# A residual block on TensorE: x's column sum computed by VectorE, and part of the low parts formed by GpSimd

## The chip, the core and the metric

The kernel runs on one core of a Trainium2 chip. Times are microseconds (us) of that core; the time before is the median of three runs, 580.67 us (580.48 to 580.83). The change is judged against it.

## What is computed

For 32 images of 64 channels, 56 x 56 pixels, float32, two 3 x 3 convolutions with folded batch norm, the input added back, and a ReLU:

```
inv = gamma * rsqrt(var + EPS)          # per channel; bn(v) = v * inv + (beta - mean * inv)
out = relu(bn(conv3x3(x, w1), g1, b1, m1, v1))
out = bn(conv3x3(out, w2), g2, b2, m2, v2)
return relu(out + x)
```

## The kernel before, in words

Rows and columns are split into even and odd ones. Two row parities times 64 channels fill the 128 partitions; the two column parities are kept as two planes of 28 x 28 values in the free dimension. The three taps of a filter row are applied with the minimal filtering trick for two outputs at a time: of each input four derived tensors are formed, and each of these goes through its own matmul with a derived filter. Two of the four are called inner (t1, the sum of the odd and even plane, and t2, their difference), two are outer (differences of neighbours). For x they are `x_inner` and `x_outer`, for the hidden image `t_inner` and `t_outer`.

Precision is kept by splitting. ScalarE copies each derived tensor to a rounded high part (`x_hi`, `ti_hi`, `h_hi`, type fp32r), then a `tensor_tensor` subtracts it from the full one to give the low part (`x_lo`, `ti_lo`, `h_lo`). TensorE does three passes: high x high, high x low filters, low x high filters. The image is done in two halves of rows; PSUM holds for each half four banks: EVEN, ODD, SUM_T1 and SUM_T2. When the inner products of a half are there, ScalarE copies the t2 sum to `z` with both signs (`copy_sum`), and VectorE's `join` writes T1 + z into EVEN and ODD at once. Then TensorE adds the outer products onto these banks, and ScalarE's ReLU reads them (`relu_hidden`, L555, for the first convolution, `relu_out`, L587, for the second). ScalarE's `residual` (L525) puts x's inner tensors into the second convolution's sum banks before the products.

The loop has one step per image. Step s does, on each engine and in a fixed order written out by hand, parts of the first convolution of image s and of the second of images s-1 and s-2. The order on TensorE in a step: for each half the inner products of conv 1 (image s) and the outer products of conv 2 (image s-2); then for each half the inner products of conv 2 (image s-1) and the outer of conv 1 (image s). The first of these, half 0 of conv 1's inner products, writes the sum bank that the join of conv 2, image s-2, half 0 reads, and waits for it (`joined[2]`). Engines talk through counting semaphores; some waits are written as `wait_ge` ahead of an instruction, and in the printed orders a row `ISA` or `REGISTER_ALU` carries such a wait or computes the count that it waits for.

VectorE in a step (lines of the kernel before): `sum_hidden` L407, join L398 (conv 2, s-2, half 1), `difference_hidden` L414, low part of t1 L430, join (conv 1, s, half 0), low part of t2, `outer_hidden` L422, `difference_x` L369 (image s+1), join (conv 1, s, half 1), `outer_x` L376, low part of h L430, inner low part of x L384, join (conv 2, s-1, half 0), outer low part of x L384.

x comes in by two ways. SyncE loads the whole image, both planes, to `x_sb`. The sum of the planes isn't computed by an engine: SyncE loads the even plane once more, to `x_inner[:, k, 0]` (`load_even`, L263), and GpSimd issues a second transfer of the odd plane which adds to it on the way (`add_odd`, L300, `accum_op=ALU.add`). There are four buffers of it (TBUFS). Only image 0's sum is made by VectorE (L354). GpSimd's computing is otherwise the prologue: scaling and summing the second layer's filters (L317, L179 to L181).

## Time and profile before

| | |
|---|---|
| median of 3 runs | 580.67 us |
| the profiled execution | 580.64 us, its span 579.0 us |
| TensorE busy | 567.1 us, 98% of the span |
| VectorE busy | 546.2 us, 94% |
| ScalarE busy | 493.1 us, 85% |
| GpSimd busy | 37.2 us, 6% |
| granted TensorE clock, mean | 0.997 |
| DMA | 79.20 MB, mean 137 GB/s |

The profile is that of one execution. Its page gives busy times, the chain of work that ended last, and groups of instructions; the trace behind it also answers for single instructions with start and duration. Consecutive instructions of an engine can overlap by up to a tenth of a microsecond, so a busy share near 100% doesn't say by itself that an engine sets the pace.

### The profile page before, as it was taken

To read this page: it belongs to the slowest core of one execution; us is meant where nothing else is said; L and a number is where in the kernel's file an instruction comes from. 1 tells how busy PE (TensorE), PEld (TensorE's weight loads), DVE (VectorE), ACT (ScalarE), POOL (GpSimd) and SP (SyncE) were. 2 spreads that over 40 slices of the span, in tenths; PEclk is the share of its full clock that TensorE was granted. 3 is DMA by queue.
4 is the path that set the end of the run, shared out by engine and by line. 5 is a ranking of instruction groups with operands and counts; after the bars stand their busy time and mean duration, and the time that the engine had idled before them with its cause. 6 is when DMAs were issued, how large, how long until landed. Compare 5 with 4: busy or idle time off the path is not lost.

```text
span 579.0 us, 9009 instructions
## 1 busy us (share of the span) xinstructions
PE 567.1 (98%) x3058; PEld 543.4 (94%) x3058; DVE 546.2 (94%) x462; ACT 493.1 (85%) x744; POOL 37.2 (6%) x44
## 2 busy tenths in 40 slices
PE   7889999999999999999999999999999999999997
PEld 4569999999999999999999999999999999999997
DVE  6799999999999999999999999999999999999985
ACT  3488888998888998888998888998888998888985
POOL 6200000000000000000000000000000000000000
PEclk9899999999999999999999999999999999999999
DMA  8733455544445544455544455544455544451112
GB/s 263 199 103 110 132 144 149 165 146 121 130 143 150 163 145 120 131 143 150 163 145 115 137 143 152 162 140 129 127 143 150 163 150 122 128 144 46 39 57 111
DMA packets 31407, 79.20 MB, mean 137 GB/s; under 512 B 2592, under 2 KB 19104, under 8 KB 31392
## 3 DMA queue, kind: packets, MB, share of 16 engines
q1 hardware_dynamic: 26784, 66.05, 31.5%
q0 software_dynamic: 4464, 12.89, 14.5%
q8 instruction: 9, 0.15, 0.1%
q10 hardware_dynamic: 144, 0.07, 0.1%
q14 instruction: 6, 0.05, 0.0%
HBM read 53.31 MB, written 25.69 MB: 136 GB/s over the span
## 4 chain that ended last, share of the span: by engine, by line
PE 93%; DVE 3%; ACT 2%; issue 1%; DMA 1%; ACTq 0%
PE psum L664 93%; DMA bn<-params_dram 1%; DVE x_lo L384 1%; ACT x_hi L515 1%; DVE psum L398 1%; DVE w_lo L198 0%; DVE t_outer L358 0%; DVE x_inner L369 0%; ACT hidden L555 0%; ACT psum L525 0%; ACT w_hi L193 0%; DVE t_inner L414 0%; DVE x_inner L354 0%; DVE x_inner L352 0%; DVE inv L337 0%
## 5 line engine op out<-in xcount | busy, mean ns | idle before, releaser
L664 PE MATMUL psum<-x_hi,w_hi 128*128 128x420 f32 x496 | 172.3, 347 | 0.5 <-DVE w_lo L198 0.5
L664 PE MATMUL psum<-x_hi,w_lo 128*128 128x420 f32 x496 | 168.8, 340 | 0.0
L664 PE MATMUL psum<-x_lo,w_hi 128*128 128x420 f32 x496 | 168.5, 340 | 0.0
L398 DVE TENSOR_TENSOR psum<-psum,z 128x784 f32<-128x784 f32 (+1 forms) x128 | 127.1, 993 | 3.6 <-ACT hidden L555 1.6
L664 PEld LDWEIGHTS psum<-x_hi,w_hi 128*128 128x128 f32 x496 | 93.1, 188 | 6.4 <-issue 4.0
L664 PEld LDWEIGHTS psum<-x_hi,w_lo 128*128 128x128 f32 x496 | 93.2, 188 | 0.8
L664 PEld LDWEIGHTS psum<-x_lo,w_hi 128*128 128x128 f32 x496 | 93.2, 188 | 0.5
L555 ACT ACTIVATE hidden<-psum,bias,half_inv 64x56 f32<-64x56 f32 (+2 forms) x128 | 84.5, 687 | 5.9 <-PE psum L664 4.7
L664 PE MATMUL psum<-h_hi,w_hi 128*128 128x392 f32 x256 | 87.3, 341 | 0.0
L664 PE MATMUL psum<-h_hi,w_lo 128*128 128x392 f32 x256 | 87.2, 341 | 0.0
L664 PE MATMUL psum<-h_lo,w_hi 128*128 128x392 f32 x256 | 87.1, 340 | 0.0
L664 PE MATMUL psum<-ti_hi,w_hi 128*128 128x392 f32 x248 | 86.7, 350 | 0.0
L664 PE MATMUL psum<-ti_lo,w_hi 128*128 128x392 f32 x248 | 84.5, 341 | 0.0
L587 ACT ACTIVATE out_sb<-psum 128x784 f32<-128x784 f32 x63 | 52.1, 827 | 38.0 <-PE psum L664 38.0
L664 PE MATMUL psum<-ti_hi,w_lo 128*128 128x392 f32 x248 | 84.1, 339 | 0.0
L525 ACT ACTIVATE psum<-x_inner 128x392 f32<-128x392 f32 x128 | 59.2, 501 | 15.1 <-DVE psum L398 15.1
L535 ACT ACTIVATE ti_hi<-t_inner 128x812 fp32r<-128x812 f32 (+2 forms) x64 | 54.6, 857 | 11.0 <-DVE t_inner L407 10.9
L430 DVE TENSOR_TENSOR ti_lo<-t_inner,ti_hi 128x812 fp32r<-128x812 f32 (+2 forms) x64 | 61.9, 970 | 0.0
L430 DVE TENSOR_TENSOR h_lo<-t_outer,h_hi 128x1624 fp32r<-128x1624 f32 (+2 forms) x33 | 59.2, 1795 | 0.4 <-ACT h_hi L535 0.4
L422 DVE TENSOR_TENSOR t_outer<-hidden 128x1624 f32<-128x1624 f32 (+2 forms) x33 | 59.2, 1793 | 0.0
L384 DVE TENSOR_TENSOR x_lo<-x_outer,x_hi 128x1568 fp32r<-128x1568 f32 x31 | 55.3, 1785 | 3.3 <-ACT x_hi L515 3.3
L376 DVE TENSOR_TENSOR x_outer<-x_sb 128x1624 f32<-128x1624 f32 x31 | 57.1, 1843 | 0.0
(62 smaller groups left out, 809.6 us busy)
## 6 DMA issues: line engine op xcount, KB each, us to landing
x_sb<-x_dram SPq DMA_DIRECT2D x32, 814.0 KB, 4.8
out_dram<-out_sb SPq DMA_DIRECT2D x63, 392.0 KB, 2.8
x_inner<-x_dram SPq DMA_DIRECT2D x31, 406.0 KB, 3.2
x_inner<-x_dram POOLq DMA_DIRECT2D x31, 406.0 KB, 5.0
out_dram<-out_sb SPq DMA_DIRECT2D x2, 196.0 KB, 2.3
z<-w_dram SPq DMA_DIRECT2D x1, 384.0 KB, 3.7
out_sb<-w_dram SPq DMA_DIRECT2D x1, 384.0 KB, 6.3
bn<-params_dram ACTq DMA_DIRECT2D x1, 68.0 KB, 3.9
```

What stands on the lines that cost most here:

```text
L376: nc.vector.tensor_tensor(x_outer[:], runs(cells, 0, XPLANE), runs(cells, 1, XPLANE), ALU.subtract).then_inc(tx_ready["outer"], 1)
L384: nc.vector.tensor_tensor(x_part(x_lo, k, places), full, x_part(x_hi, k, places).bitcast(F32), ALU.subtract).then_inc(xlo_ready[which], 1)
L398: nc.vector.tensor_tensor(psum[:, half, EVEN:ODD + 1, 0:width], t1, z[:, half, :, 0:width], ALU.add).then_inc(joined[conv], 1)
L422: nc.vector.tensor_tensor(t_outer[:, :, rows], hid_cols[:, :, rows, 0:WQ], hid_cols[:, :, rows, 1:WQ + 1], ALU.subtract).then_inc(th_ready ...
L430: nc.vector.tensor_tensor(lo, full, hi.bitcast(F32), ALU.subtract).then_inc(hlo_ready[which], 1)
L515: nc.scalar.activation(x_part(x_hi, k, places), full, ACT.Copy).then_inc(xhi_ready[which], 1)
L525: ins = nc.scalar.activation(psum[:, half, bank, 0:width].rearrange("p (j q) -> p j q", q=WQ), x_full("inner", k)[0][:, i, j0:j1], ACT.Cop ...
L535: nc.scalar.activation(hi, full, ACT.Copy).then_inc(hhi_ready[which], 1)
L555: return nc.scalar.activation(hid_data[rows, :, pairs, 0:WQ], sums[rows], ACT.Relu, bias=bias[rows, 0:1], scale=half_inv[rows, 0:1])
L587: nc.scalar.activation(out_sb[:, half], psum[:, half, EVEN:ODD + 1, 0:(j1 - j0) * WQ], ACT.Relu).then_inc(out_ready, 1)
L664: ins = nc.tensor.matmul(sums, w[:, i, far, :], t[:, j0:j1, 0:WQ], start=not onto and at == 0, stop=at == len(todo) - 1, skip_group_check= ...
```

## The change

x's sum for each image is computed by VectorE (`sum_x`, 784 elements per partition), behind the join of conv 1, half 1, and ahead of `outer_x`. Both transfers that made it are gone. In exchange VectorE forms only rows 0 to 14 of the outer low parts of x and of h (for h, but for the last two images). The rest, 13 rows of x (364 elements) and 14 rows of h (392), is done by GpSimd in four instructions per image, one for each of the two outer tensors ("place") of x and of h. Before each, GpSimd waits for the semaphores that one of VectorE's joins waits for and for the VectorE instruction ahead of that join (`beside_join`). TensorE, and VectorE where it overwrites the full tensor, wait for the pieces (`x_piece`, `h_piece`).

```diff
-            def load_even(n, k):
-                sp.dma_start(x_inner[:, k, 0], x_rows[n][:, 0:RUN]).then_inc(even_in[k], 16)
...
-                if not isinstance(s, int) or 0 <= s < N - 3:
-                    wait(sp, res_ready, 2 * s)
-                    load_even(s + 3, (k + 3) % 4)
...
-            def add_odd(n, k):
-                pool.wait_ge(even_in[k], landed(n, k))
-                odd = x_rows[n][:, XPLANE + 1:XPLANE + 1 + RUN]
-                pool.dma_start(x_inner[:, k, 0], odd, accum_op=ALU.add).then_inc(summed[k], 16)
...
+            def x_part_low(n, k, place):
+                rows = slice(HALF1[1][0], NQ)
+                pool.wait_ge(xhi_ready["outer"], n)
+                pool.tensor_tensor(x_lo[:, k % 2, place, rows], x_full("outer", k)[0][:, place, rows],
+                                   x_hi[:, k % 2, place, rows].bitcast(F32), ALU.subtract).then_inc(x_piece, 1)
+            def hidden_part_low(n, b, place):
+                rows = slice(HALF1[1][0], NP)
+                pool.wait_ge(hhi_ready["outer"], n + 1)
+                pool.tensor_tensor(h_lo[:, b, place, rows], t_outer[:, place, rows],
+                                   h_hi[:, b, place, rows].bitcast(F32), ALU.subtract).then_inc(h_piece, 1)
+            def beside_join(conv, n, half, earlier, count):
+                pool.wait_ge(earlier, count)
+                pool.wait_ge(z_ready[conv], 2 * n + half + 1)
+                pool.wait_ge(inner[conv], 2 * (2 * n + half) + 2)
...
             def step(s, k):
-                if there_is(s, s + 2):
-                    add_odd(s + 2, (k + 2) % 4)
+                now, last, store = there_is(s, s), there_is(s, s - 1), there_is(s, s - 2)
+                if is_step(s, N) or is_step(s, N + 1):
+                    return
+                if store:
+                    beside_join(2, s - 2, 1, th_ready["t1"], s)
+                    pool.wait_ge(hidden_ready, 2 * (s - 1) + 2)
+                    hidden_part_low(s - 2, k % 2, 1)
+                if now and not is_step(s, 0):
+                    if not is_step(s, 1):
+                        beside_join(1, s, 0, hlo_ready["t1"], s - 1)
+                        pool.wait_ge(out_ready, 2 * (s - 2) + 1)
+                    x_part_low(s, k, 0)
+                    if not is_step(s, 1):
+                        beside_join(1, s, 1, th_ready["outer"], s)
+                        pool.wait_ge(out_ready, 2 * (s - 2) + 2)
+                    x_part_low(s, k, 1)
+                if last and not is_step(s, N - 1):
+                    beside_join(2, s - 1, 0, xlo_ready["inner"], s + 1)
+                    pool.wait_ge(hidden_ready, 2 * s + 1)
+                    hidden_part_low(s - 1, (k + 1) % 2, 0)
...
+            def sum_x(n, k):
+                cells = runs(x_sb[:, k % XBUFS], 0, XPLANE + 1).rearrange("p s (j c) -> p s j c", c=WQ + 1)
+                nc.vector.tensor_tensor(x_full("inner", k)[0][:, 0], cells[:, 0, :, 0:WQ], cells[:, 1, :, 0:WQ],
+                                        ALU.add).then_inc(sum_ready, 1)
...
                 wait(dve, xlo_ready["outer"], n - 1)
+                wait(dve, x_piece, 2 * (n - 1))
...
+                rows = slice(0, NQ if which == "inner" else HALF1[1][0])
                 dve.wait_ge(xhi_ready[which], n)
-                nc.vector.tensor_tensor(x_part(x_lo, k, places), full,
-                                        x_part(x_hi, k, places).bitcast(F32),
+                nc.vector.tensor_tensor(x_part(x_lo, k, places)[:, :, rows], full[:, :, rows],
+                                        x_part(x_hi, k, places)[:, :, rows].bitcast(F32),
...
                 wait(dve, hlo_ready["outer"], n)
+                wait(dve, h_piece, 2 * (N - 2) if is_step(n, N - 1) else 2 * n)
...
+                if which == "outer" and half is None and not is_step(n, N - 2):
+                    rows = slice(0, HALF1[1][0])
+                    full, hi, lo = full[:, :, rows], hi[:, :, rows], lo[:, :, rows]
...
                     difference_x(1, 1)
+                    sum_x(1, 1)
                     join(1, 0, 0, (2, -2))
                     outer_x(1, 1)
...
                 if ahead:
+                    sum_x(s + 1, ka)
                     outer_x(s + 1, ka)
                 if last:
...
                 if which == "inner":
-                    act.wait_ge(summed[k], landed(n, k))
+                    act.wait_ge(sum_ready, n + 1)
...
                 pe.wait_ge(joined[conv], 2 * n + half + 1)
+                if half == 1 and conv == 1 and not is_step(n, 0):
+                    pe.wait_ge(x_piece, 2 * n)
+                if half == 1 and conv == 2 and not is_step(n, N - 2) and not is_step(n, N - 1):
+                    pe.wait_ge(h_piece, 2 * n + 2)
```

Line numbers shift: the join is L421 after the change, the sum of the hidden planes L430, its difference L437, t_outer L446, the low parts L457 (hidden) and L407 (x), x's difference L384, x_outer L398. The first place to see is VectorE in a step of the loop, from the outer hidden tensor to the outer low part of x. Before:

```order
L422 TENSOR_TENSOR t_outer<-hidden 128x1624 [waits hlo_outer]
L366 ISA
L369 TENSOR_TENSOR x_inner<-x_sb 128x28x28 [waits res_ready,x_in0]
L393 REGISTER_ALU
L394 ISA [waits z1_ready]
L398 TENSOR_TENSOR psum<-psum,z 128x2x392 [waits out_ready,inner1]
L376 TENSOR_TENSOR x_outer<-x_sb 128x1624 [waits xlo_outer]
L430 TENSOR_TENSOR h_lo<-t_outer,h_hi 128x1624 [waits hhi_outer]
L384 TENSOR_TENSOR x_lo<-x_inner,x_hi 128x1568 [waits xhi_inner]
L398 TENSOR_TENSOR psum<-psum,z 128x2x392 [waits hidden_ready,inner2,z2_ready]
L384 TENSOR_TENSOR x_lo<-x_outer,x_hi 128x1568 [waits xhi_outer]
```

After:

```order
L446 TENSOR_TENSOR t_outer<-hidden 128x1624 [waits h_piece,hlo_outer]
L381 ISA
L384 TENSOR_TENSOR x_inner<-x_sb 128x28x28 [waits res_ready,x_in0]
L416 REGISTER_ALU
L417 ISA [waits z1_ready]
L421 TENSOR_TENSOR psum<-psum,z 128x2x392 [waits out_ready,inner1]
L390 TENSOR_TENSOR x_inner<-x_sb 128x28x28
L398 TENSOR_TENSOR x_outer<-x_sb 128x1624 [waits x_piece,xlo_outer]
L457 TENSOR_TENSOR h_lo<-t_outer,h_hi 128x2x420 [waits hhi_outer]
L407 TENSOR_TENSOR x_lo<-x_inner,x_hi 128x1568 [waits xhi_inner]
L421 TENSOR_TENSOR psum<-psum,z 128x2x392 [waits hidden_ready,inner2,z2_ready]
L407 TENSOR_TENSOR x_lo<-x_outer,x_hi 128x2x420 [waits xhi_outer]
```

One instruction is new, the sum (L390), between the join of half 1 and x_outer. The two outer low parts are 2 x 420 elements long in place of 1624 and 1568, and t_outer and x_outer wait for pieces too. No instruction changed its place among the others.

The second place is GpSimd's queue in the loop. Before, two steps:

```order
L300 ISA [waits even_in0]
L300 DMA x_inner<-x_dram 128x812
L298 REGISTER_ALU
L300 ISA [waits even_in1]
L300 DMA x_inner<-x_dram 128x812
```

After, one step and the beginning of the next (z1, z2: `z_ready`; hlo_t1, th_outer, xlo_inner, th_t1: the VectorE instruction ahead of the join):

```order
L315 ISA [waits z2_ready,th_t1]
L308 TENSOR_TENSOR h_lo<-t_outer,h_hi 128x392 [waits hhi_outer,hidden_ready,inner2]
L314 ISA [waits hlo_t1]
L315 ISA [waits z1_ready]
L301 TENSOR_TENSOR x_lo<-x_outer,x_hi 128x364 [waits xhi_outer,out_ready,inner1]
L314 REGISTER_ALU [waits th_outer]
L315 ISA [waits z1_ready]
L301 TENSOR_TENSOR x_lo<-x_outer,x_hi 128x364 [waits xhi_outer,out_ready,inner1]
L313 REGISTER_ALU
L308 TENSOR_TENSOR h_lo<-t_outer,h_hi 128x392 [waits hidden_ready,inner2,hhi_outer,z2_ready,xlo_inner]
```

Where a step had one transfer, it has four tensor_tensor instructions, with rows that wait or compute counts between them.

## Rows read from the trace of the kernel before

**Rows 1.** The page, busy time of the engines.
```profile
PE 567.1 (98%) x3058; PEld 543.4 (94%) x3058; DVE 546.2 (94%) x462; ACT 493.1 (85%) x744; POOL 37.2 (6%) x44
```

**Rows 2.** Windows table, one step: us, then each engine's busy time.
```profile
core 0: us, PE busy (x) PEld busy (x) DVE busy (x) ACT busy (x) POOL busy (x), PEclk, DMA share, GB/s
302.50:319.83 17.33, 17.33 (x97) 16.99 (x97) 16.87 (x15) 15.32 (x25) 0.82 (x2) 1.00 0.47 127
```

**Rows 3.** Timeline, TensorE: first matmuls of steps (start us, us).
```profile
41.91 0.46 PE L664 MATMUL psum<-x_hi,w_hi 128*128 128x420 f32 x1 [0.53 <-DVE w_lo L198]
...
302.50 0.43 PE L664 MATMUL psum<-x_hi,w_hi 128*128 128x420 f32 x1
...
337.22 0.43 PE L664 MATMUL psum<-x_hi,w_hi 128*128 128x420 f32 x1
...
545.50 0.42 PE L664 MATMUL psum<-x_hi,w_hi 128*128 128x420 f32 x1
```

**Rows 4.** Timeline, VectorE, one step and the next one's join.
```profile
305.42 0.98 DVE L398 TENSOR_TENSOR psum<-psum,z 128x784 f32<-128x784 f32 x1
...
306.31 1.00 DVE L414 TENSOR_TENSOR t_inner<-hidden 128x812 f32<-128x812 f32 x1
...
308.16 1.04 DVE L398 TENSOR_TENSOR psum<-psum,z 128x840 f32<-128x840 f32 x1
...
310.02 1.85 DVE L422 TENSOR_TENSOR t_outer<-hidden 128x1624 f32<-128x1624 f32 x1
...
312.66 0.98 DVE L398 TENSOR_TENSOR psum<-psum,z 128x784 f32<-128x784 f32 x1
...
321.87 1.00 DVE L407 TENSOR_TENSOR t_inner<-hidden 128x812 f32<-128x812 f32 x1 [0.43 <-ACT hidden L555]
...
336.10 0.98 DVE L398 TENSOR_TENSOR psum<-psum,z 128x784 f32<-128x784 f32 x1
```

**Rows 5.** Timeline, ScalarE, the same step.
```profile
311.36 0.83 ACT L587 ACTIVATE out_sb<-psum 128x784 f32<-128x784 f32 x1 [0.41 <-PE psum L664]
...
312.08 1.56 ACT L535 ACTIVATE h_hi<-t_outer 128x1624 fp32r<-128x1624 f32 x1
...
315.31 1.52 ACT L515 ACTIVATE x_hi<-x_inner 128x1568 fp32r<-128x1568 f32 x1
...
320.37 1.37 ACT L555 ACTIVATE hidden<-psum,bias,half_inv 64x56 f32<-64x56 f32 x2
```

**Rows 6.** VectorE's groups by form: count | busy us, mean ns | idle before.
```profile
L430 DVE TENSOR_TENSOR h_lo<-t_outer,h_hi 128x1624 fp32r<-128x1624 f32 x31 | 57.2, 1846 | 0.4 <-ACT h_hi L535 0.4
...
L384 DVE TENSOR_TENSOR x_lo<-x_outer,x_hi 128x1568 fp32r<-128x1568 f32 x31 | 55.3, 1785 | 3.3 <-ACT x_hi L515 3.3
...
L369 DVE TENSOR_TENSOR x_inner<-x_sb 128x784 f32<-128x784 f32 x31 | 30.6, 987 | 0.0
...
L430 DVE TENSOR_TENSOR h_lo<-t_outer,h_hi 128x840 fp32r<-128x840 f32 x1 | 1.0, 1027 | 0.0
```

**Rows 7.** Timeline, GpSimd, prologue.
```profile
6.97 0.53 POOL L306 TENSOR_TENSOR inv<-inv,bn 128x66 f32<-128x66 f32 x1 [4.61 <-DVE inv L342]
...
8.04 0.20 POOL L308 TENSOR_TENSOR bias<-bn,inv 128x2 f32<-128x2 f32 x1
...
9.85 1.84 POOL L317 TENSOR_TENSOR out_sb<-out_sb,half_inv 128x768 f32<-128x768 f32 x1
...
14.01 1.58 POOL L180 TENSOR_TENSOR w_mat<-out_sb 128x256 f32<-128x256 f32 x1
...
15.56 1.45 POOL L181 TENSOR_TENSOR w_mat<-out_sb 128x256 f32<-128x256 f32 x1
```

**Rows 8.** Timeline, VectorE, prologue.
```profile
6.66 0.23 DVE L342 TENSOR_TENSOR inv<-inv,tmp 128x66 f32<-128x66 f32 x1
...
9.87 3.47 DVE L358 TENSOR_TENSOR t_outer<-x_sb 128x1568 f32<-128x1568 f32 x1
...
14.94 1.49 DVE L369 TENSOR_TENSOR x_inner<-x_sb 128x784 f32<-128x784 f32 x1
...
16.35 1.03 DVE L398 TENSOR_TENSOR psum<-psum,z 128x840 f32<-128x840 f32 x1
```

More of the change, by code:

```diff
@@ L110, in residual_block @@
         wlo_ready = {1: sem("wlo1"), 2: sem("wlo2")}
-        first_sum = sem("first_sum")
-        even_in = [sem(f"even_in{i}") for i in range(TBUFS)]
-        summed = [sem(f"summed{i}") for i in range(TBUFS)]
+        sum_ready = sem("sum_ready")
+        x_piece, h_piece = sem("x_piece"), sem("h_piece")
         tx_ready = {"inner": sem("tx_inner"), "outer": sem("tx_outer")}
@@ L199, in low_weights @@
                               ALU.subtract).then_inc(wlo_ready[conv], 1)
-        def landed(n, k):
-            return (n - k) * (16 // TBUFS) + (16 if k else 0)
         def runs(cells, first, step):
@@ L259, in store @@
                 sp.dma_start(out_rows[n][:, half], out_sb[:, half]).then_inc(stored[half], 16)
-            def load_even(n, k):
-                sp.dma_start(x_inner[:, k, 0], x_rows[n][:, 0:RUN]).then_inc(even_in[k], 16)
             sp.dma_start(w_raw[1], w1).then_inc(w_in[1], 16)
             load(sp, 0, 0)
-            load_even(1, 1)
             sp.dma_start(w_raw[2], w2).then_inc(w_in[2], 16)
             load(sp, 1, 1)
-            load_even(2, 2)
             def step(s, k):
@@ L309, in _ @@
             pool.tensor_tensor(bias[:], bn[:, 2 * COLS:2 * COLS + 2], bias[:], ALU.subtract).then_inc(bias_ready, 1)
-            add_odd(1, 1)
             pool.wait_ge(w_in[2], 16)
@@ L354, in first_x @@
                 nc.vector.tensor_tensor(planes[:, 0], cells[:, 0, :, 0:WQ], cells[:, 1, :, 0:WQ],
-                                        ALU.add).then_inc(first_sum, 1)
+                                        ALU.add).then_inc(sum_ready, 1)
                 cells = x_sb[:, 0, 0:2 * XPLANE].rearrange("p (s r) -> p s r", s=2)[:, :, 0:RUN] \
@@ L370, in difference_x @@
                                         ALU.subtract).then_inc(tx_ready["inner"], 1)
+            def sum_x(n, k):
+                cells = runs(x_sb[:, k % XBUFS], 0, XPLANE + 1).rearrange("p s (j c) -> p s j c", c=WQ + 1)
+                nc.vector.tensor_tensor(x_full("inner", k)[0][:, 0], cells[:, 0, :, 0:WQ], cells[:, 1, :, 0:WQ],
+                                        ALU.add).then_inc(sum_ready, 1)
             def outer_x(n, k):
                 wait(dve, xlo_ready["outer"], n - 1)
+                wait(dve, x_piece, 2 * (n - 1))
                 cells = x_sb[:, k % XBUFS]
@@ L743, in step @@
                             pe.wait_ge(prep[1], 3)
-                            pe.wait_ge(first_sum, 1)
+                            pe.wait_ge(sum_ready, 1)
                         sum_products(1, half, 1, SUM_T1, whole_passes(1, 1), False).then_inc(inner[1], 1)
```

## The prediction

> **What bounds the kernel now.** The first view is the page's list of busy times: TensorE is busy for 98% of the span [rows 1]. A change that touches no matmul then looks as if it could do nothing. The windows table of one step of the loop in the middle says more: TensorE is busy all the time and VectorE for 16.87 of 17.33 us [rows 2]. Two engines are full, so the question is which one waits, and TensorE's waits are too short to show as idle time. They are found in the starts of the matmuls. The first matmul of a step starts at 41.91 in step 2 and at 545.50 in step 31 [rows 3]: 29 steps, 503.59 us, 17.365 us a step.
>
> Then I read VectorE, ScalarE and TensorE side by side and look for the chain that closes on itself. It spans two steps:
> - step start 302.50 [rows 3]; TensorE reaches the end of the half that ScalarE's output ReLU waits for, and that ReLU starts at 311.36;
> - ScalarE then has no idle time until its ReLU of 320.37 ends at 321.74 [rows 5];
> - VectorE starts on the hidden image at 321.87 and works without idle time up to the join that starts at 336.10 and ends at 337.08 [rows 4];
> - the step after next starts at 337.22 [rows 3], 0.14 later. That matmul overwrites the bank that the join read.
>
> 337.22 - 302.50 = 34.72 = 2 x 17.36. So the loop runs at the length of this chain, not at TensorE's rate. What lengthens VectorE's part of it by D adds D/2 to each step. What shortens VectorE's work outside it adds and saves nothing.
>
> A second, shorter loop lies next to it: VectorE's t_outer (310.02 + 1.85 = 311.87) releases ScalarE's h_hi, which starts at 312.08 because the output ReLU before it is in the way [rows 4, 5]. About 0.2 us of delay is free there.
>
> **The change part by part.** *VectorE's own work.* One more sum of 784 elements: 987 ns like its twin, of which 0.09 overlaps a neighbour (a join of 0.98 is followed after 306.31 - 305.42 = 0.89) [rows 4, 6]: +0.90. h_lo falls from 1624 to 840 elements: 1846 to 1027 ns, -0.82. The outer x_lo falls from 1568 to 840: 1785 to about 1030 ns, -0.76 [rows 6]. In sum -0.68 us of load per step. But the sum and h_lo lie ahead of the join that closes the chain, and the outer x_lo behind it, where VectorE waits for the hidden ReLU anyway. On the chain it is +0.90 - 0.82 = +0.08.
>
> *The four pieces on GpSimd* (392, 364, 364, 392 elements). GpSimd does hardly anything in the loop, so its own time is free. What it does to VectorE isn't. In the prologue both work at once. GpSimd's scaling starts at 9.85 and ends at 11.69; VectorE's t_outer, started at 9.87, took 3.47 us, where 1568 elements take 1.785 [rows 6 to 8]: 1.69 longer, that is the overlap of 1.82 less 0.13. VectorE's x_inner at 14.94 took 1.49 instead of 0.97 (the mean of the other 30, from [rows 6]) and GpSimd's sum before it ended at 15.59: 0.65 of overlap, 0.52 longer, again 0.13 less. But the join at 16.35 took 1.03, its usual length (1.04 at 308.16), while GpSimd worked from 16.43 to 17.01 [rows 4, 7, 8]. So a VectorE operation on two SBUF tensors waits for GpSimd, and a join, which reads PSUM and z, doesn't. A piece is free as long as it ends within its join, plus 0.13.
>
> Does it? GpSimd's speed: after VectorE let it go at 14.94 + 1.49 = 16.43, 256 elements were done at 17.01, 2.27 ns each [rows 7, 8]. 364 elements are 0.83 us, 392 are 0.89. An operation of two elements took 0.20 [rows 7], so a fixed 0.10 to 0.20 comes on top; I take 0.15. When does it start? Its first wait is for the VectorE operation ahead of the join, which ends 0.08 after the join starts (16.43 and 16.35). From VectorE's end to GpSimd's start it took 6.97 - 6.89 = 0.08 [rows 7, 8]; VectorE itself took 0.13 behind ScalarE (321.87 after 321.74) [rows 4, 5]. The piece has three to four further waits queued behind the first, already met; I take 0.12, between 0.08 and 0.30. A piece of h then ends 0.08 + 0.12 + 0.15 + 0.89 = 1.24 after the join's start. The next VectorE operation, a difference or low part of two SBUF tensors each time, starts at 0.89 and bears 0.13: 0.22 to 0.24 late. A piece of x at the 784-element join: 1.18 - 1.02 = 0.17. At the longer join (1.04): 0.10. From both sides: 0.16, 0.09 and 0 with the small values, 0.46, 0.40 and 0.29 with the large.
>
> Three of the four lie on the chain (h beside 305.42, x beside 308.16, x beside 312.66): 0.24 + 0.10 + 0.17 = 0.51. The fourth, beside the join of 336.10, lies behind the chain and is hidden in VectorE's wait. Before t_outer there are 0.34, of which some 0.2 are free; that loop, 17.16 + 0.34 = 17.50, stays below the other.
>
> The chain grows by 0.08 + 0.51 = 0.59, the step by 0.295, to 17.66; over 29 steps 8.6 us. With the small values: 0.33, 4.8 us. With the large: 1.23, 17.8 us.
>
> The Trainium skill (SBUF — State Buffer, Who interferes with whom) says the same of who waits, but that the second one to issue "fully blocks until the first finishes". By that rule the 0.13 are not borne and each of the three blocks is 0.13 longer: 29 x 0.39 / 2 = 5.7 us more, about 597. The trace disagrees by those 0.13, twice, so the sum above stands without it.
>
> *The transfers.* The loads of the even half and GpSimd's accumulating loads go. TensorE waits for none of them in the loop, and VectorE's operations are no shorter when they don't run; nothing. ScalarE's inner x_hi now waits for VectorE's sum, which ends 0.34 + 0.17 + 0.88 after 313.64, at 315.0; ScalarE comes to that x_hi at 315.31 [rows 5]. Hidden by 0.3. New waits: TensorE needs a piece at the second half of the outer products, some 5 us after the x piece and 2 to 3 after the h piece; outer_x on VectorE stands a sum behind its piece. Nobody waits there. SP's queue loses waits and gets none.
>
> *The start.* Image 1's sum comes directly behind x_inner (14.94). GpSimd's last filter sum, which until now ran beside the join of 16.35, now blocks that sum by 0.52: 0.88 + 0.52 = 1.4, all on the way to TensorE's outer products. In step 1 the two x pieces have no join beside them, come together with VectorE's outer x_lo and hold VectorE up by about 0.75 each, less the 0.76 saved: +0.7. A last 0.3 beside the filters' low part. Sum 2.4; from both sides 0.9 (only the sum) to 3.5. Nothing at the end, where pieces and sums have stopped.
>
> Sum: 580.64 (span 579.0 and 1.64 around it; the median of the runs shown is 580.67) + 8.6 + 2.4 = 591.6.
>
> **The rivals.**
> 1. *The join covers the pieces.* GpSimd is quick to start and has no fixed cost (2.27 ns x 364 is well under a join). Then the chain grows by 0.08 only: 29 x 0.04 = 1.2, with a start of 0.9 to 2.4: 583. For it speaks that 0.22 us per piece rests on two numbers of 0.1 each; against it, that the small measured values already give 0.33.
> 2. *GpSimd is late.* Its queue walks through register arithmetic and waits before each piece; if that takes 0.35 and more, blocks are 0.35 to 0.45 each: 29 x (0.08 + 1.05) / 2 = 16.4, with 3 at the start 600. Were the pieces not beside the joins at all, that is if the change doesn't do what it says, VectorE's load would be 16.87 - 0.68 + 3.44 = 19.63 a step, 2.27 more: about 648.
> 3. *Faster: VectorE's load decides.* If VectorE's total and not the two-step chain sets the step, 0.68 saved is worth something, as soon as blocks stay under 0.17 a piece. TensorE's own floor is near: its first matmul starts 0.07 to 0.14 behind the join, and it can gain at most some 0.11 a step, 29 x 0.11 = 3.2; with 0.9 at the start 578.4. For it: VectorE is 97% busy [rows 2]. Against it: it is idle 0.43 before 321.87, each step, waiting for ScalarE [rows 4].
>
> **How the numbers follow.** Forecast 0.62, rival 1 0.15, rival 2 0.13 (0.03 of it far out), rival 3 0.10. The likeliest case alone is 585 to 598: from 4.8 with 0.9 to 14 with 3. The range takes in rival 1 and the near part of rival 2: 582.5 to 601. A measurement of this kernel tells about 0.2% (1.2 us) from no change: slower 0.85 (forecast, rivals 1 and 2 but for some 0.05), same 0.07, faster 0.08.
>
> **What would show it.** In the profile after: steps of 17.66 between first matmuls; joins of unchanged length; the operation behind each of the four joins 0.1 to 0.25 longer than its form (the differences of x and h, the low part of t2 above 1.00, the outer x_lo above 1.03); VectorE's idle time ahead of the hidden sum at about 0.7 us instead of 0.43 (17.66, less 16.92 - 0.68 + 0.74); pieces of about 1.0 us starting 0.2 behind a join. Wrong if those operations keep their lengths (rival 1), or if the idle time before the hidden sum doesn't grow while the step shrinks (rival 3). The time would also be wrong if the chain had a partner that I take for free, h_hi above all.

## The result, and the profile after

The changed kernel takes 592.35 us (592.04 to 592.53, 4 runs) against 580.61 (580.48 to 580.83, 4 runs): 1.0206 times as long, 95% interval 1.0192 to 1.022. Forecast were 591.6, range 582.5 to 601.

The page of the changed kernel, busy times, against [rows 1]:

```profile
PE 571.4 (97%) x3058; PEld 543.2 (92%) x3058; DVE 547.2 (93%) x493; ACT 494.7 (84%) x744; POOL 141.3 (24%) x135
```

As many matmuls as before, almost the same VectorE time (547.2 against 546.2), and 11.1 us more span. The busy times don't tell where it went. TensorE's first matmuls of step 2, 3, 26 and 31 do (timeline, start and duration; against [rows 3]):

```profile
43.28 0.46 PE L693 MATMUL psum<-x_hi,w_hi 128*128 128x420 f32 x1 [0.71 <-DVE w_lo L197]
...
60.76 0.43 PE L693 MATMUL psum<-x_hi,w_hi 128*128 128x420 f32 x1
...
468.73 0.43 PE L693 MATMUL psum<-x_hi,w_hi 128*128 128x420 f32 x1 [0.15 <-DVE psum L421]
...
555.92 0.43 PE L693 MATMUL psum<-x_hi,w_hi 128*128 128x420 f32 x1
```

The span of 590.1 against 579.0 falls in three parts. Up to step 2: 43.28 against 41.91, +1.37. The 29 steps to step 31: 512.64 us, 17.677 each against 17.365, +9.05. After it: 34.18 against 33.50, +0.68. And the 29 are of two kinds. Of the 24 in the loop, the first (step 2) took 17.48 and the other 23 average 17.738 ((468.73 - 60.76) / 23); the five behind the loop, whose instructions are written out, average only 17.438.

VectorE's groups by form in the changed kernel (count | busy us, mean ns | idle before), against [rows 6]:

```profile
L457 DVE TENSOR_TENSOR ti_lo<-t_inner,ti_hi 128x812 fp32r<-128x812 f32 x60 | 64.2, 1070 | 0.0
...
L437 DVE TENSOR_TENSOR t_inner<-hidden 128x812 f32<-128x812 f32 x31 | 40.2, 1298 | 0.0
L407 DVE TENSOR_TENSOR x_lo<-x_outer,x_hi 128x840 fp32r<-128x840 f32 x31 | 38.2, 1232 | 3.1 <-ACT x_hi L544 3.1
L421 DVE TENSOR_TENSOR psum<-psum,z 128x840 f32<-128x840 f32 x32 | 33.1, 1034 | 0.7 <-PE psum L693 0.6
L457 DVE TENSOR_TENSOR h_lo<-t_outer,h_hi 128x840 fp32r<-128x840 f32 x31 | 31.6, 1021 | 0.0
L430 DVE TENSOR_TENSOR t_inner<-hidden 128x812 f32<-128x812 f32 x31 | 31.4, 1014 | 22.5 <-ACT hidden L584 22.5
...
L390 DVE TENSOR_TENSOR x_inner<-x_sb 128x784 f32<-128x784 f32 x31 | 30.3, 976 | 0.0
```

The hidden difference (L437) takes 1298 ns where it took 995 (it was 1.00 in [rows 4]). The outer x_lo takes 1232 where the h_lo of the same 840 elements takes 1021. The low parts of t1 and t2 (L457) average 1070 against 997, and single rows show that those of t1 are all 0.99, so t2's are longer by twice the difference. The joins kept their length. The new sum (L390) is not longer than its twin. Behind three of four joins something blocks VectorE, behind one nothing. VectorE's idle time before the hidden sum rose to 22.5 us in all, where it was 12.4; that is 0.73 a step in the loop against 0.44.

The pieces on GpSimd, one step of the changed kernel, and VectorE's rows around them:

```profile
325.86 1.03 POOL L308 TENSOR_TENSOR h_lo<-t_outer,h_hi 128x392 fp32r<-128x392 f32 x1 [5.49 <-DVE x_lo L407]
329.99 1.04 POOL L308 TENSOR_TENSOR h_lo<-t_outer,h_hi 128x392 fp32r<-128x392 f32 x1 [3.10 <-DVE t_inner L430]
333.15 0.90 POOL L301 TENSOR_TENSOR x_lo<-x_outer,x_hi 128x364 fp32r<-128x364 f32 x1 [2.12 <-DVE ti_lo L457]
337.00 1.32 POOL L301 TENSOR_TENSOR x_lo<-x_outer,x_hi 128x364 fp32r<-128x364 f32 x1 [2.95 <-DVE t_outer L446]
```

```profile
328.56 1.01 DVE L430 TENSOR_TENSOR t_inner<-hidden 128x812 f32<-128x812 f32 x1 [0.77 <-ACT hidden L584]
329.49 0.97 DVE L421 TENSOR_TENSOR psum<-psum,z 128x784 f32<-128x784 f32 x1
330.37 1.53 DVE L437 TENSOR_TENSOR t_inner<-hidden 128x812 f32<-128x812 f32 x1
...
336.59 0.96 DVE L384 TENSOR_TENSOR x_inner<-x_sb 128x784 f32<-128x784 f32 x1
337.48 0.97 DVE L421 TENSOR_TENSOR psum<-psum,z 128x784 f32<-128x784 f32 x1
338.36 0.96 DVE L390 TENSOR_TENSOR x_inner<-x_sb 128x784 f32<-128x784 f32 x1
```

The piece at 329.99 starts 0.42 after VectorE's hidden sum ended (329.57). It ends at 331.03, which is 0.66 after the hidden difference began; that one is longer by 0.53, again 0.13 less. The last piece is the exception: it has 1.32 us on record, more than any other, and blocks nobody. It started at 337.00, before its join, found the port (so the shared access to SBUF is called here, for which the two engines wait for each other) taken by x's difference (336.59 to 337.55) and was through 0.77 us after that. A piece that stands ready doesn't pay the time from VectorE's signal, and it is through 0.13 sooner than one of the same size that starts on a free port (0.90). It comes in so early because it waits for t_outer, not for the instruction directly ahead of its join (the diff shows `th_outer`; the order has the x difference between them), which the forecast missed.

### The profile page after: what moved, and what is told of

Its sections match the earlier page's. It is cut to its first block, busy times and chain, and to the rows that moved or that the text cites. A ratio compares the mean times of both kernels' runs of the same rounds, so it can differ in the third digit from the quotient of the medians.

```text
span 590.1 us, 9394 instructions
## 1 busy us (share of the span) xinstructions
PE 571.4 (97%) x3058; PEld 543.2 (92%) x3058; DVE 547.2 (93%) x493; ACT 494.7 (84%) x744; POOL 141.3 (24%) x135
## 4 chain that ended last, share of the span: by engine, by line
PE 49%; DVE 22%; issue 15%; ACT 13%; DMA 1%; DVEq 1%; ACTq 0%
PE psum L693 49%; DVE psum L421 6%; ACT hidden L584 4%; DVE t_outer L446 4%; ACT x_hi L544 3%; DVE ti_lo L457 3%; DVE x_outer L398 2%; ACT z L577 1%; DVE x_inner L390 1%; ACT z L578 1%; ACT psum L554 1%; DVE h_lo L457 1%; DVE x_lo L407 1%; DVE t_inner L437 1%; DMA bn<-params_dram 1%
## 5 line engine op out<-in xcount | busy, mean ns | idle before, releaser
L421 DVE TENSOR_TENSOR psum<-psum,z 128x784 f32<-128x784 f32 (+1 forms) x128 | 126.4, 987 | 3.5 <-ACT hidden L584 1.6
L308 POOL TENSOR_TENSOR h_lo<-t_outer,h_hi 128x392 fp32r<-128x392 f32 x60 | 62.3, 1038 | 258.1 <-DVE x_lo L407 172.5
L301 POOL TENSOR_TENSOR x_lo<-x_outer,x_hi 128x364 fp32r<-128x364 f32 x62 | 68.0, 1097 | 162.0 <-ACT out_sb L616 72.9
L457 DVE TENSOR_TENSOR ti_lo<-t_inner,ti_hi 128x812 fp32r<-128x812 f32 (+2 forms) x64 | 66.3, 1039 | 0.0
L446 DVE TENSOR_TENSOR t_outer<-hidden 128x1624 f32<-128x1624 f32 (+2 forms) x33 | 59.0, 1787 | 0.0
L398 DVE TENSOR_TENSOR x_outer<-x_sb 128x1624 f32<-128x1624 f32 x31 | 56.9, 1837 | 0.0
```

The costliest lines, as they stand in the source:

```text
L301: pool.tensor_tensor(x_lo[:, k % 2, place, rows], x_full("outer", k)[0][:, place, rows], x_hi[:, k % 2, place, rows].bitcast(F32), ALU.sub ...
L308: pool.tensor_tensor(h_lo[:, b, place, rows], t_outer[:, place, rows], h_hi[:, b, place, rows].bitcast(F32), ALU.subtract).then_inc(h_piec ...
L398: nc.vector.tensor_tensor(x_outer[:], runs(cells, 0, XPLANE), runs(cells, 1, XPLANE), ALU.subtract).then_inc(tx_ready["outer"], 1)
L421: nc.vector.tensor_tensor(psum[:, half, EVEN:ODD + 1, 0:width], t1, z[:, half, :, 0:width], ALU.add).then_inc(joined[conv], 1)
L446: nc.vector.tensor_tensor(t_outer[:, :, rows], hid_cols[:, :, rows, 0:WQ], hid_cols[:, :, rows, 1:WQ + 1], ALU.subtract).then_inc(th_ready ...
L457: nc.vector.tensor_tensor(lo, full, hi.bitcast(F32), ALU.subtract).then_inc(hlo_ready[which], 1)
```

## The experiments

The two theories: **A**, the step is set by chains through VectorE's closing join, and GpSimd's pieces lengthen them by holding the port behind a join. **B**, something else does it: VectorE's total load, the sum as such, or the port from the pieces' mere length. All runs are compared with the kernel before on the same chip; its median was 580.74 beside the first four, 580.61 and 580.66 beside the others. "Step" is the mean over the 29 from step 2 to 31.

**No pieces.** GpSimd's `run(pool, step)` and the waits on `x_piece` and `h_piece` are taken out.

```diff
+                nc.gpsimd.memset(x_lo[:, b, 0:2, HALF1[1][0]:NQ].bitcast(F32), 0.0).then_inc(blank, 1)
+                nc.gpsimd.memset(h_lo[:, b, 0:2, HALF1[1][0]:NP].bitcast(F32), 0.0).then_inc(blank, 1)
...
-            run(pool, step)
...
-                    pe.wait_ge(x_piece, 2 * n)
...
-                    pe.wait_ge(h_piece, 2 * n + 2)
```

TensorE's work stays the same: GpSimd sets the rows that the pieces would form to zero once, at the start, so this kernel leaves out those low parts.

> The changed kernel, with the four GpSimd pieces of each image left out (the rows of the low parts that they would form stay zero) and all waits on them gone; VectorE's sum and its shortened low parts stay. Theory (two-step chain plus blocks by the shared port): only +0.08 us is left on the chain, the step goes from 17.68 to 17.40 us, 583 to 584.5 us in all; the operations behind the joins return to their plain lengths (hidden difference 1.00, low part of t2 0.99, outer x_lo 1.03) and VectorE idles above 1.0 us before the hidden sum. Rival (VectorE's total load sets the step): load is 0.68 below before, so 578 to 580. Rival (the sum on VectorE costs it all, pieces nothing): stays at 592.

Measured 584.14 us (ratio 1.0062, 1.0048 to 1.0076), step 17.433, hidden difference 0.995, outer x_lo 1.025, VectorE idle 1.09 a step before the hidden sum. As A said; B's 578 and 592 are both out. The pieces cost 8.2 of the 11.7 us, the sum with the shortened low parts and without the transfers the other 3.5. Note that VectorE idles more than twice as long as before the change (1.09 against 0.41 over the same 29 steps), and the kernel is still slower.

**The queue written out.** The loop with its registers made GpSimd late?

```diff
-            run(pool, step)
+            for s in range(N + 2):
+                step(s, s % 4)
```

> The changed kernel with GpSimd's steps written out with constants instead of a loop with register arithmetic; same instructions, same waits. Theory (a piece blocks VectorE because GpSimd's queue needs time for register waits after VectorE's signal): the loop's 23 steps take the 17.44 us that the written-out last steps take now, not 17.74: about 585.5 us; hidden difference 1.18 everywhere, low part of t2 0.99. Rival (the blocks come from the pieces' own length, whatever the queue): 592, lengths as now.

Measured 587.77 us (1.0121, 1.0105 to 1.0136), step 17.482. VectorE's groups in this run:

```profile
L458 DVE TENSOR_TENSOR ti_lo<-t_inner,ti_hi 128x812 fp32r<-128x812 f32 x60 | 59.5, 991 | 0.0
...
L438 DVE TENSOR_TENSOR t_inner<-hidden 128x812 f32<-128x812 f32 x31 | 37.2, 1199 | 0.0
```

t2's low part is at its plain length, the hidden difference 0.2 above it, as in the last steps of the changed kernel. The same arithmetic and the same waits, only with constants: 4.6 us less. The steps alone say more: without pieces they are 0.244 shorter than in the changed kernel, with constants 0.195. So four fifths of what the pieces cost in the steps comes from the way in which GpSimd's queue waits; the rest fits the start delay and the fixed part.

The trace of the changed kernel shows it for h's first piece of a step. Where the wait for VectorE's hidden sum stands on the piece itself, the piece starts 0.08 us after the sum's end. Where this wait is an entry of its own in the queue and one more entry stands between it and the piece, it is 0.25. Where four entries lie between the sum's end and the piece (at 329.60, 329.69, 329.79 and 329.88, three of them with computed counts), it is 0.42. VectorE's hidden difference is 1.18, 1.35 and 1.53 us long in these cases. The loop's branch is not in the way: it comes 3.4 us ahead of the latest of these pieces. With constants every such piece starts 0.08 behind.

The time is 2.3 above the expectation. 1.6 of it lies ahead of step 2, whose first matmul came at 44.89 instead of 43.28. There TensorE's granted clock was at half (1.2 GHz, the lower of its two levels) for 10.2 us in all, where the changed kernel's trace has 3.4 us of it (windows table of this run: from, to, us; then busy time of TensorE, its weight loads, VectorE, ScalarE and GpSimd; granted clock; DMA share and GB/s):

```profile
16.94:23.77 6.83, 5.13 (x8) 2.73 (x9) 5.88 (x5) 1.51 (x1) 0.00 (x0) 0.50 0.36 118
34.01:37.42 3.41, 3.41 (x8) 1.76 (x6) 3.41 (x4) 3.32 (x5) 0.00 (x0) 0.50 0.00 0
```

The rest is steps of 17.48 instead of 17.44.

**Early release.** The three other pieces are let go early, like x's second.

```diff
-                    beside_join(2, s - 2, 1, th_ready["t1"], s)
...
+                    pool.wait_ge(xlo_ready["outer"], s)
...
-                        beside_join(1, s, 0, hlo_ready["t1"], s - 1)
...
+                        pool.wait_ge(th_ready["t2"], s)
...
-                    beside_join(2, s - 1, 0, xlo_ready["inner"], s + 1)
...
+                    pool.wait_ge(hlo_ready["outer"], s)
```

> The changed kernel; three of the four pieces wait for less: x's first piece for the instruction two ahead of its join, h's second (behind the closing join) likewise, h's first for the outer x_lo of the step before, so that it falls into VectorE's idle time. The piece then stands ready when the port comes free, as x's second piece does now. Theory: blocks behind the joins vanish, at most 0.1 to 0.3 us is left ahead of the hidden sum: step 17.42 to 17.55, 584 to 588 us. Rival (an early piece takes the port from the operation ahead of the join and holds it for its whole length): that operation grows by 0.8 to 0.9 us each, over 600 us.

Measured 585.26 us (1.0086, 1.0072 to 1.0101), step 17.438, the same as with no pieces at all. GpSimd in this run:

```profile
302.36 2.52 POOL L308 TENSOR_TENSOR h_lo<-t_outer,h_hi 128x392 fp32r<-128x392 f32 x1 [3.79 <-DVE h_lo L454]
305.89 1.03 POOL L308 TENSOR_TENSOR h_lo<-t_outer,h_hi 128x392 fp32r<-128x392 f32 x1 [1.00 <-DVE x_lo L404]
309.82 1.59 POOL L301 TENSOR_TENSOR x_lo<-x_outer,x_hi 128x364 fp32r<-128x364 f32 x1 [2.90 <-DVE t_inner L434]
```

And VectorE's outer x_lo beside the first of them:

```profile
302.20 1.78 DVE L404 TENSOR_TENSOR x_lo<-x_inner,x_hi 128x1568 fp32r<-128x1568 f32 x1
303.90 0.97 DVE L418 TENSOR_TENSOR psum<-psum,z 128x784 f32<-128x784 f32 x1
304.78 1.02 DVE L404 TENSOR_TENSOR x_lo<-x_outer,x_hi 128x840 fp32r<-128x840 f32 x1
```

The piece "lasts" 2.52 us on record, is held up by the inner x_lo (until 303.98), ends at 304.88 and delays nothing. That is 0.90 after the port came free, where such a piece takes 1.04 from a free start. Of the 1.1 us to the run without pieces the traces place 0.73 in the start (step 2's first matmul at 43.35 against 42.62), where step 1's pieces have no join, and 0.15 in the steps.

**x's second piece late.** The one piece that was free is made like the others.

```diff
-                        beside_join(1, s, 1, th_ready["outer"], s)
+                        beside_join(1, s, 1, *((th_ready["outer"], s) if is_step(s, N - 1)
+                                               else (tx_ready["inner"], s + 2)))
```

> The changed kernel; only x's second piece is moved to wait for the instruction directly ahead of its join (x's difference) as the other three do. Theory: it starts about 0.3 us later relative to the port's release, the sum of x behind the join is blocked by 0.2 to 0.3 us, on the chain: 23 to 29 steps by half of it, 594.5 to 597 us. Rival (half a block does not reach the step since VectorE has 0.8 us idle): 592.35.

Measured 596.27 us (1.0278, 1.0264 to 1.0292), step 17.802. The sum of x went from 976 to 1213 ns:

```profile
L391 DVE TENSOR_TENSOR x_inner<-x_sb 128x784 f32<-128x784 f32 x31 | 37.6, 1213 | 0.0
```

So the block can be made as well as removed, which is A's point. The step grew by 0.125. That it is half of 0.24 proves nothing: the average of t1's and t2's low parts fell from 1070 to 1032 at the same time, which is 0.08 less block on t2's, so 0.16 net gave 0.125.

**The sum alone.** VectorE's whole low parts, no pieces; only the sum is new.

```diff
-                rows = slice(0, NQ if which == "inner" else HALF1[1][0])
+                rows = slice(0, NQ)
...
-                    rows = slice(0, HALF1[1][0])
-                    full, hi, lo = full[:, :, rows], hi[:, :, rows], lo[:, :, rows]
...
-            run(pool, step)
...
```

> Half of the change alone: VectorE's sum in place of the two transfers; VectorE forms the whole low parts itself, GpSimd has no pieces. Theory: +0.90 us on the chain is +0.45 a step, and VectorE's load (16.92 + 0.90 = 17.82) becomes the floor: steps of 17.82 to 17.9, 594 to 597 us. Rival (what costs is the port only): about 584, as without pieces.

Measured 607.93 us (1.0483, 1.0467 to 1.05), step 18.244. Both theories missed; A by 11 us. VectorE, one step of this run:

```profile
302.60 1.00 DVE L451 TENSOR_TENSOR ti_lo<-t_inner,ti_hi 128x812 fp32r<-128x812 f32 x1
304.09 1.04 DVE L419 TENSOR_TENSOR psum<-psum,z 128x840 f32<-128x840 f32 x1 [0.49 <-ACT out_sb L610]
```

VectorE is overloaded and yet waits 0.49, at the join of the first convolution, for ScalarE's output ReLU of half 0. That is a second chain, of one step: step start, outer products of half 0, this ReLU, this join, VectorE's work to the closing join, next step start. What lies between the two joins counts in it in full: 17.36 + 0.90 = 18.26. In the kernel before the two chains were equally long. This is its ReLU (timeline):

```profile
307.23 0.83 ACT L587 ACTIVATE out_sb<-psum 128x784 f32<-128x784 f32 x1 [0.81 <-PE psum L664]
```

It ends at 308.06, and the join of 308.16 [rows 4] starts 0.10 behind it; over the 29 steps the gap is 0.11 on average and never under 0.10, and it is the same 0.11 in the run with the sum alone, where this chain sets the step. The forecast read only the other chain.

**The sum off the chain.** The sum of image s+2 behind the outer x_lo at the end of step s; x's first and h's second piece released early.

```diff
-                    sum_x(s + 1, ka)
...
+                if there_is(s, s + 2) and not (isinstance(s, int) and s > N - 3):
+                    k2 = (k + 2) % 4
+                    dve.wait_ge(x_in[k2 % XBUFS], until(s + 2, k2))
+                    wait(dve, res_ready, 2 * (s + 2 - TBUFS) + 2)
+                    sum_x(s + 2, k2)
```

> The changed kernel with the sum of image s+2 behind the outer x_lo at the end of step s, off the chain, and with early release of x's first and h's second piece. Same work on every engine. Theory: the chain is 0.82 - 0.2 to 0.3 shorter than before the change, so TensorE's floor (17.05 of matmuls and some 0.2 of waits) sets the step: 17.25 to 17.30, and 578.5 to 580 us with the longer start. Rival (VectorE's load or the pieces set the step, not the place of the sum): 17.43 as with early release alone, 585.

Measured 593.85 us (1.0244, 1.0227 to 1.0261), step 17.733: the expectation was wrong by 14 us. VectorE and GpSimd:

```profile
322.58 1.03 DVE L455 TENSOR_TENSOR h_lo<-t_outer,h_hi 128x840 fp32r<-128x840 f32 x1
324.08 2.30 DVE L405 TENSOR_TENSOR x_lo<-x_inner,x_hi 128x1568 fp32r<-128x1568 f32 x1 [0.47 <-ACT x_hi L548]
```

```profile
323.69 1.05 POOL L308 TENSOR_TENSOR h_lo<-t_outer,h_hi 128x392 fp32r<-128x392 f32 x1 [2.98 <-DVE h_lo L455]
```

VectorE came too early to the inner x_lo and had to wait for ScalarE's x_hi. In that idle time the piece, released early, got the port and held the inner x_lo up by 0.5 on the closing join's chain. In these runs early release is free only where VectorE's operation ahead of the join has already started.

**A cheaper start.** As that, with image 1's sum behind the first join and image 1's outer low part whole on VectorE.

```diff
+                    join(1, 0, 0, (2, -2))
                     sum_x(1, 1)
-                    join(1, 0, 0, (2, -2))
...
-                if now and not is_step(s, 0):
+                if now and not is_step(s, 0) and not is_step(s, 1):
...
```

> As the run with the sum off the chain, and in the prologue image 1's sum stands behind the first join, and image 1's outer low part is formed by VectorE whole. Theory: the start costs nothing any more, the first matmul of step 2 comes at 42.0 instead of 43.3 us: 1.3 us less than the run before, 577 to 578.7. Rival (the start is hidden anyway): no difference between the two.

Measured 591.35 us (1.0186, 1.0168 to 1.0205), step 17.729: 2.5 less than the run before at the same step. So the difference lies in the start, but it isn't all the start's work. TensorE's granted clock differs there (windows tables, first the run before, then this one; the 0.50 and 1.00 are the granted clock):

```profile
19.21:22.62 3.41, 3.41 (x7) 1.74 (x6) 3.28 (x3) 0.00 (x0) 0.00 (x0) 0.50 0.50 151
32.86:36.27 3.41, 3.41 (x8) 1.81 (x6) 3.41 (x4) 3.32 (x5) 0.00 (x0) 0.50 0.00 0
```

```profile
0.00:45.00 45.00, 35.70 (x132) 24.61 (x133) 37.54 (x38) 26.13 (x40) 13.13 (x15) 1.00 0.32 112
```

The run before had two stretches of 3.41 us at 1.2 GHz, this one none. By the mean clock, such stretches come and go between executions of one kernel: this kernel's two executions at a mean clock of 1.000 took 589.61 and 590.40, its three at 0.996 to 0.997 took 591.35 to 591.48. One stretch is thus worth about 1.4 us here. The median of the run before was measured at 0.994 and this one at 0.997, which is one stretch less. An estimate from these numbers leaves some 1.1 of the 2.5 us for the cheaper start, near the 1.3 expected. It is loose: between two executions of the next run the same step of the clock (1.000 to 0.997) was worth 0.4 us (589.96 and 590.32). The absolute value missed with the step, as above.

**The pieces alone.** The transfers are kept, the pieces released as in the last two.

```diff
-                    sum_x(s + 1, ka)
...
+                if there_is(s, s + 2):
+                    add_odd(s + 2, (k + 2) % 4)
```

> The other half alone: the transfers make x's sum as before the change, GpSimd forms the four pieces (two with early release) and issues its transfer behind them. Theory: the chain is shortened by 0.82 less one block of 0.2 to 0.3, TensorE's floor sets the step, 17.25 to 17.30: 577.5 to 579 us. The transfers themselves are worth nothing. Rival (transfers cost TensorE or VectorE something, or GpSimd's issuing delays pieces): 580.7 or more, steps of 17.37 and up.

Measured 591.78 us (1.0195, 1.0178 to 1.0213), step 17.724, so this expectation missed by 13 us for the same reason. Again a 2.32 us inner x_lo behind 0.45 of idle time. It did not tell the transfers from the rest, since one block covered both.

**h's second piece not early.** In the two variants, back to waiting for the inner x_lo:

```diff
-                    pool.wait_ge(hlo_ready["outer"], s)
+                    beside_join(2, s - 1, 0, xlo_ready["inner"], s + 1)
+                    pool.wait_ge(hidden_ready, 2 * s + 1)
```

> As the run with the sum off the chain and the cheaper start, except that h's second piece waits again for the inner x_lo, as in the change. Theory formed after the last four: there VectorE came 0.44 us early to the inner x_lo (it waits for ScalarE's inner x_hi), the early piece took the port in that idle time and blocked the inner x_lo by 0.54, on the way to the closing join. With the piece behind it, the inner x_lo is 1.78 again and starts behind x_hi, the step falls to 17.27 to 17.35: 577.5 to 580 us. Rival (steps of 17.73 had another cause, such as the port in general): 591.

> GpSimd's pieces with the transfers kept, h's second piece waiting for the inner x_lo as in the change, x's first released early. Theory: as above, inner x_lo back to 1.78, step 17.27 to 17.35, 577.5 to 580. Rival (GpSimd's issuing of transfers or the transfers cost): steps above 17.4, 582 and more.

Measured 583.13 us (1.0042, 1.0028 to 1.0056) and 583.60 us (1.0048, 1.0033 to 1.0062); steps 17.435 and 17.437. The inner x_lo is 1.79 in both. The cause was found, the size not wholly: the last five steps take 17.24 to 17.28, the loop's 17.28 to 17.65. Each step above 17.5 is one in which ScalarE's h_hi waits about 0.2 us for VectorE's t_outer; the others in the loop stay at 17.28 to 17.46. The step is the same with the transfers and no sum on VectorE as without them and the sum at the end of VectorE's step. So no cost of the transfers shows in the loop, and taking them away gains nothing.

**And the queue written out.**

```diff
-            run(pool, step)
+            for s in range(N + 2):
+                step(s, s % 4)
```

> The same with GpSimd's queue written out with constants. Theory: h's first piece blocks by 0.18 instead of 0.28 on average and t_outer no longer delays ScalarE's h_hi in two steps of four; 17.27: equal to the run before or up to 1.5 us less. Rival (GpSimd's register waits no longer matter as the chain has slack): exactly equal.

Measured 579.47 us (578.61 to 580.48, 12 runs), ratio 0.9984, interval 0.9974 to 0.9994; step 17.338 against 17.365. That is the only version faster than the kernel before, by 0.16% of the medians. Part of this is the granted clock: 6 of its 12 executions were at a mean of 0.999 or more, but 4 of the 17 of the kernel before. At 0.999 and more the medians are 578.79 and 579.43, below that 580.36 and 580.72, so the kernel itself is faster by 0.4 to 0.6 us, some 0.1%. On the version before (583.13) it gained 3.7 us of the medians, and 2.9 to 3.0 at equal clock, of which 2.8 are in the steps. That is more than expected, and the rival's "equal" is out. ScalarE's h_hi now waits for t_outer once, for 0.07 us, where it waited 12 times, 2.5 us in all.

**The sum alone, off the chain.**

```diff
-                    sum_x(s + 1, ka)
...
+                    sum_x(s + 2, k2)
...
```

> The sum alone (no pieces, whole low parts by VectorE), at the end of the step behind the outer x_lo. Theory: the one-step loop (output ReLU of half 0, join of the first convolution's half 0 up to the closing join) is as long as before the change, so the sum is no longer paid there; but VectorE's load is 17.82 a step and nothing can hide it: 17.82 to 17.9, 594 to 597 us, against 607.9 with the sum on the chain. Rival (the 18.24 of the sum alone were load, with waits that no order removes): 607.

Measured 592.00 us (1.0201, 1.0187 to 1.0215), step 17.693, 2 us under the expectation. VectorE's idle time before the hidden sum is under 0.01 a step: here its load is the bound. Against 607.93 with the same instructions in the other place: 15.9 us for one instruction's position.

## Why the prediction came out right

The chain and the blocks behind the joins are as forecast, but 591.6 against 592.35 is closer than the working was. The steps came out 0.4 us longer in sum (9.05 against 8.6), the start 1.0 shorter and the end 0.7 longer, and these nearly cancel. That part is luck.

*The bound, right but incomplete.* That the loop runs at the length of a chain through VectorE's closing join, not at the load, is shown: without pieces VectorE has less load and more idle time than before and the kernel is slower; the same sum in another place differs by 15.9 us. But there are two such chains of equal length. The rule "what is added counts half" holds as long as the two-step one is the longer. For the sum alone it fails. In the change itself it cost little: +0.08 of the sum less the shorter h_lo was counted as 0.04, and the run without pieces shows 17.433 - 17.365 = 0.068, so it counts nearly in full there.

*The blocks.* The mechanism is as predicted, row for row, the 0.13 included. Their sizes, by place: hidden difference 0.24 forecast, 0.30 measured; t2's low part 0.10 and 0.16; x's sum 0.17 and 0; outer x_lo 0.24 and 0.22, without effect. On the chain 0.51 and 0.46. The sum is near because errors offset each other, again luck. Missed was that x's second piece is released early, though the printed order had it. And the queue's waits: a uniform 0.12 was taken, where the hidden difference in the loop is 1.53, 1.35, 1.18 and 1.18 us long, by the position in the loop's turn of four, and 1.18 behind the loop.

*t_outer.* Forecast as just below the limit ("h_hi above all"). In the step with the longest block it isn't: ScalarE's h_hi waits for t_outer in 6 cases, 1.5 us in all, and TensorE then waits for ScalarE. These 6 are the longest steps of all, 17.96 to 18.06. The list of TensorE's waits in the changed kernel (us in total, times, longest), where before only 2 waits of 2.3 us stood for ScalarE's residual:

```profile
PE psum L693 <- DVE psum L421: 5.6, 10, 3.9
PE psum L693 <- ACT psum L554: 3.7, 7, 2.1
```

Outside the start these are 9 waits of 1.7 us and 5 of 0.9 us; the kernel before has none there. So 8.6 us were forecast for the 29 steps and 9.05 measured: (0.08 + 0.46) / 2 x 29 = 7.8 from the chain, 0.8 more if the 0.08 adds 0.068 to a step and not 0.04, and the rest fits t_outer's path; how they divide was not tested.

*The start, mis-sized.* 2.4 forecast, 1.37 measured, with one stretch of 3.4 us at half the granted clock in either trace (17.48 to 20.89 before, 19.66 to 23.08 after). The block of image 1's sum is there (1.49 us instead of 0.98), and step 1's blocks too (1.26 and 1.69 for two operations of 1.00). But what came before was quicker:

```profile
9.57 3.13 DVE L373 TENSOR_TENSOR t_outer<-x_sb 128x1568 f32<-128x1568 f32 x1
...
15.71 1.49 DVE L390 TENSOR_TENSOR x_inner<-x_sb 128x784 f32<-128x784 f32 x1
17.12 1.03 DVE L421 TENSOR_TENSOR psum<-psum,z 128x840 f32<-128x840 f32 x1
```

The parameters landed 0.3 us sooner, and GpSimd, without a transfer to issue, began its scaling 1 us earlier and blocked VectorE's first t_outer for less (3.13 against 3.47 in [rows 8]). The join comes 0.77 later instead of 1.4. The two stretches lie in different places, and the clock's share of the 1.37 was not separated.

*The end, missed.* "Nothing at the end" is right for the engines: ScalarE's last output copy ends 30.92 us after step 31's first matmul, 30.90 before. The last 0.66 are behind it, in the last stores. DMA issues (count, KB each, median us to landing), before 2.3:

```profile
out_dram<-out_sb SPq DMA_DIRECT2D x2, 196.0 KB, 2.8
```

All the kernels without the transfers show the longer end (34.08 to 34.21 us from step 31's first matmul to the span's end), the kernel before and the two that keep them 33.4 to 33.5. Why is open.

*The rivals.* Cover by the joins: true for one piece of four, and it would have been 585 with all of them (early release). Late GpSimd: partly true, the waits in its queue are 4.6 us (5.7 in the steps alone). VectorE's load: out, except where the load itself was raised. By the forecast's working, the Trainium skill's reading that the second one is blocked until the first has finished would have given 597; the words stand on its page SBUF — State Buffer in the section Summary: rules for kernel authors. The traces disagree with it by the 0.13: in about 600 cases in ten kernels the VectorE operation was longer by the overlap less 0.12 to 0.14.

## What to carry to other kernels

Before work is moved off a full engine, look for the chain that closes on itself and for its twin a few tenths beside it: what lies between its ends counts, what lies behind them is free, and relief on one member only brings forward the wait for the next. An engine that shares a port is best queued while the other already holds it. It then runs the moment the port is free; released by the last signal before the gap it comes late by its queue's waits and its own start, and released into idle time it blocks the one that idle time was for. Where a queue needs to be prompt, write its waits with constants.

## What the runs showed of the hardware

- GpSimd's `tensor_tensor` and a VectorE `tensor_tensor` of two SBUF operands exclude each other for their whole length, less 0.12 to 0.14 us (about 600 cases in the ten kernels with pieces; overlaps under 0.13 us lengthened nothing); a VectorE operation of one PSUM and one SBUF operand kept its length (1.03 to 1.04, and 0.97) beside GpSimd.
- Of GpSimd: 392 elements took 1.04 us and 364 took 0.90 from a free start; a piece of 364 that stood ready was done 0.77 after the port came free, one of 392 0.90 after it. So GpSimd too is spared some 0.13 us when it waits for the port.
- Entries with waits in GpSimd's queue, some on computed counts, delayed an instruction when VectorE's signal found them still ahead of it: it started 0.08 us after VectorE's end with none of them, 0.25 with two, 0.42 with four. VectorE's block behind it was 0.18, 0.35 and 0.53 us.
- A record on GpSimd includes the time for which it waits for the port: 2.52 us for 392 elements.
- TensorE's granted clock was at half (1.2 GHz) for between 0 and 10.2 us of the first 45 us, by the traces of the different kernels, and the mean clock differs between executions of one kernel too. The kernel before took 579.28 to 579.68 us at a mean of 0.999 to 1.000, and 580.39 to 581.27 at 0.996 to 0.997.
